# Tiles of the second norm, and the norm's small operations, in forms with two tensor sources on VectorE

## The chip, the core and the metric

The kernel runs on one core of a Trainium2 chip. The metric is the device time of one execution in microseconds (us), here the median of three: 321.2 us before the change, between 321.14 and 321.3. TensorE is called PE, VectorE DVE, ScalarE ACT, GpSimd POOL and SyncE SP.

## The reference, cut to what matters

Input: x (2 batches, 1024 tokens, 256 wide), a context of 64 tokens for each batch, and the weights of a gated cross-attention (16 heads of 64) and of a mixture of 8 experts, of which 2 are used for each batch.

```
x = x + tanh(g_xattn) * attention(layernorm(x), context)     # softmax over 64 context tokens, then Wo, bo
y = layernorm(x)                                             # mean, var over the 256 columns, eps 1e-5
logits = mean over tokens(y) @ gate_w ; the two best experts of each batch, weights renormalised
x = x + tanh(g_ffn) * sum over the 2 experts of w * (gelu(y @ w1[e] + b1[e]) @ w2[e] + b2[e])
```

## The kernel before, in words

All is float32 in the inputs. Each product on PE is split in a high and a low half (`_hi`, `_lo`, type fp32r) and done as three matmuls into the same sum (lines 1153 to 1155). The tokens lie in 16 tiles of 128; tile t of x is `xt[:, t, :]`, 128 partitions by 256 columns.

Every engine has its own list of instructions, in an order written out by hand, and the lists are tied by semaphores. The attention runs as a software pipeline of steps s (function `step` on each engine). In one step PE transposes the probabilities of tile s-2 (L1238), transposes a tile of y where there is one (L1326), computes the scores of tile s, and multiplies the transposed probabilities with the folded value weights (`ps<-vw`). From s = 3 on the residual of tile s-3 is added to x on DVE (L949), and `bn_stats` takes its statistics (L954).

POOL has three jobs in these steps: it multiplies the probabilities with the reciprocal of their sum (L504, two halves, PE waits for them before L1238), it normalises a later tile of x in two passes over `xs` (L522, L524), and it refines reciprocal square roots by Newton's iteration for most groups of tiles (`newton`, L470 to L476, thirteen small instructions, each waited for by the next). In steps 7, 11 and 15 this iteration stands ahead of L504 in POOL's list, in steps 1 and 4 behind it.

The change touches two functions of DVE:

- `norm` (its `0 in parts` block, lines 762 to 768, and the first guess at line 770) turns the two halves of `bn_stats` into mean and variance of a group of tiles: instructions on 128x4 or 128x8 elements. It is called seven times: three times for x (four, four and eight tiles) and four times for y (four tiles each). `link` puts a wait behind an instruction: DVE goes on only when that instruction has signalled. Behind `norm`, POOL is told to begin the Newton iteration, except in the first call for x and the last for y, where DVE does the iteration itself (L774 to L776).
- `y_tile` (line 969) writes y of one tile, (x - mean) * rstd, as one `tensor_scalar` with mean and rstd as per-partition scalars. It is called for the eight tiles of batch 0: one at the end of each of steps 7 to 10, two each at the end of steps 11 and 12. PE's transposes of that tile (L1326) wait for it. The eight tiles of batch 1 are done by POOL in two passes (L535, L538), and are not touched.

The only other `tensor_scalar` of this kind on DVE in the steps, `xn` at line 883, keeps its form. Neither do the experts' loops change: there DVE splits the gelu's output in two halves (L1112, L1114) and the next expert's weights (L1048, L1053).

Of the kernel before, what the change touches and what calls it, by code (L numbers as in the profile page):

```python
# [5 lines left out]
def gated_cross_attention_moe_kernel(nc, x, xT, ctx_tokens, g_xattn, g_ffn, Wq, Wk, Wv, Wo, bo,  # L6
# [5 lines left out]
    ALU = mybir.AluOpType  # L12
# [4 lines left out]
    P = 128  # L17
    B, M, D = ctx_tokens.shape
    S = out.shape[0] // B
    HD = 2 * Wv.shape[-1]  # L20
    DH = 64
    H = HD // DH
    E, _, F = w1.shape
    TOP = 2
    NT = B * S // P
# [10 lines left out]
    EPS = 1e-5  # L36
# [4 lines left out]
    def x_block(b, t0, t1):  # L41

        first = next(n for n, (part, u0, u1) in enumerate(_X_BLOCKS) if part == b and u0 <= t0 and t1 <= u1)
        assert _X_BLOCKS[first] == (b, t0, t1)
        start = sum(P * (u1 - u0) * D for _, u0, u1 in _X_BLOCKS[:first])
        return x[start:start + P * (t1 - t0) * D].rearrange("(p t d) -> p t d", p=P, d=D)
# [6 lines left out]
    def place(name, shape, dtype=f32, at=None):  # L53
        size = 4
        for n in shape[1:]:
            size *= n
        offset = cursor[0] if at is None else at[0]
        t = nc.alloc_sbuf_tensor_at(name, shape, dtype, offset=offset)
        (cursor if at is None else at)[0] = offset + (size + 31) // 32 * 32
        return t  # L60


    xt = place("xt", [P, NT, D])
# [3 lines left out]

    stats2 = stats1
    mean1 = place("mean1", [P, NT])
    rstd1 = place("rstd1", [P, NT])  # L70
    mean2 = place("mean2", [P, NT])
    rstd2 = place("rstd2", [P, NT])
# [67 lines left out]
    yb = place("yb", [P, 2, D], at=first3)  # L140
# [35 lines left out]
    with stack:  # L176
        ps = stack.enter_context(nc.psum_tensor("ps", [P, 8, BANK], f32))

        def sem(name):
            return stack.enter_context(nc.semaphore(name))  # L180
# [25 lines left out]
        y_ready, yT_done, yhi_ready, ylo_ready = (  # L206
            sem(n) for n in ("y_ready", "yT_done", "yhi_ready", "ylo_ready"))
        rep_ready, logits_done, idx_ready, gap_ready, gap_done, sel_ready = (
            sem(n) for n in ("rep_ready", "logits_done", "idx_ready", "gap_ready", "gap_done", "sel_ready"))
        stat_out, stat_in, xT_raw, xT_ready = (sem(n) for n in ("stat_out", "stat_in", "xT_raw", "xT_ready"))  # L210
        y_rstd, x_rstd, xn_by_dve, w1_first = sem("y_rstd"), sem("x_rstd"), sem("xn_by_dve"), sem("w1_first")
        staged_w1 = [sem("staged_w1_0"), sem("staged_w1_1")]
        staged_half = [sem("staged_half_0"), sem("staged_half_1")]
# [151 lines left out]
        def wait_pos(eng, s, v):  # L365

            if v > 0:
                eng.wait_ge(s, v)
# [375 lines left out]
        def _(dve):  # L744
            ln = [0]

            def link(ins):

                ln[0] += 1
                ins.then_inc(ln_step, 1)  # L750
                dve.wait_ge(ln_step, ln[0])

            def norm(t0, t1, mean, rstd, var, parts=range(4)):


                tiles, n = slice(t0, t1), t1 - t0
                me, ce, mo, co = (stats1[:, tiles, i] for i in (1, 2, 4, 5))
                m, r = mean[:, tiles], rstd[:, tiles]
                v, d, u = var[:, tiles], dm[:, 0:n], nu[:, 0:n]
                tt, ts, stt = nc.vector.tensor_tensor, nc.vector.tensor_scalar, nc.vector.scalar_tensor_tensor  # L760
                if 0 in parts:
                    tt(d, me, mo, ALU.subtract)
                    tt(m, me, mo, ALU.add)
                    link(tt(v, ce, co, ALU.add))
                    ts(m, m, 0.5, None, ALU.mult)
                    tt(d, d, d, ALU.mult)
                    link(ts(v, v, 1.0 / D, EPS, ALU.mult, ALU.add))
                    link(stt(v, d, 0.25, v, ALU.mult, ALU.add))

                    link(ts(r.bitcast(i32), v.bitcast(i32), -0.5, float(0x5F3759DF), ALU.mult, ALU.add))  # L770
                for part in (1, 2, 3):
                    if part in parts:

                        link(stt(u, v, -0.5, r, ALU.mult, ALU.mult))  # L774
                        link(tt(u, u, r, ALU.mult))
                        link(stt(r, u, 1.5, r, ALU.add, ALU.mult))  # L776
# [12 lines left out]
            def x_norm(i):  # L789

                t0, t1 = X_PARTS[i]
                dve.wait_ge(stats_done, stats_of[t1 - 1])
                norm(t0, t1, mean1, rstd1, ve_x, range(4) if i == 0 else (0,))
                dve.sem_inc(guess_ready, 1)

            def group(kind, i):
                n = number[(kind, i)]
                bank = ps[:, GRP_BANK[(kind, i)], :]
                if kind == "ctxT":
                    dve.wait_ge(grp_done, n + 1)  # L800
                    nc.vector.tensor_copy(ctxT[:, :, :], bank[:, 0:D].rearrange("p (k i) -> p k i", k=KD)).then_inc(grp_dve, 1)
                if kind == "vT":
                    dve.wait_ge(grp_done, n + 1)
                    nc.vector.tensor_copy(vT_sb[:, 4 * i:4 * i + 4, :, :].rearrange("p m b j -> p (m b j)"),
                                          bank).then_inc(grp_dve, 1)
                if kind == "A":
                    dve.wait_ge(grp_hi, HI_AT[(kind, i)])
                    nc.vector.tensor_tensor(a_part(a_lo, i), bank.rearrange("p (m b x) -> p m b x", m=4, b=B),
                                            as_f32(a_part(a_hi, i)), ALU.subtract).then_inc(grp_dve, 1)
                if kind == "VW":  # L810
                    dve.wait_ge(tg_ready, 1)
                    dve.wait_ge(grp_hi, HI_AT[(kind, i)])
                    nc.vector.scalar_tensor_tensor(vw[:, 2 * i:2 * i + 2, D:2 * D],
                                                   bank.rearrange("p (m n) -> p m n", m=2), tg[:, 0:1],
                                                   as_f32(vw[:, 2 * i:2 * i + 2, 0:D]), ALU.mult,
                                                   ALU.subtract).then_inc(grp_dve, 1)
# [13 lines left out]
                                        ALU.subtract).then_inc(xlo_ready, 1)  # L830

            nc.vector.memset(warm_w[:, :], 0.0).then_inc(warm_ready, 1)
            dve.sem_inc(hlo_ready, FREE_GELS)
            group("ctxT", 0)
            x_stats(0, range(0, 2))
# [12 lines left out]
            def step(s, par):  # L848
# [82 lines left out]
                for y in (Y_WITH_X.get(s + 1), Y_AFTER.get(s + 1)):  # L931
                    if y is not None:
                        y_tile(y)
# [24 lines left out]
            def y_guess(i):  # L958

                t0, t1 = Y_PARTS[i]  # L960
                dve.wait_ge(stats_done, stats_of[("x1", t1 - 1)])
                norm(t0, t1, mean2, rstd2, ve_y, range(4) if i == 3 else (0,))
                dve.sem_inc(guess_ready, 1)

            def y_tile(t):

                dve.wait_ge(y_rstd, t // 4 + 1)
                wait_pos(dve, yT_done, t - 1)
                nc.vector.tensor_scalar(yb[:, t % 2, :], xt[:, t, :], mean2[:, t:t + 1], rstd2[:, t:t + 1],
                                        ALU.subtract, ALU.mult).then_inc(y_ready, 1)  # L970

            def y_low(t, bank, c0, until):

# [550 lines left out]
```

## Time and profile before

| | |
|---|---|
| median of 3 runs | 321.2 us (321.14 to 321.3) |
| the profiled execution | 321.67 us, of which 319.7 us are the profiled span |
| PE busy | 313.2 us, 98% of the span |
| DVE busy | 236.5 us, 74%, 563 instructions |
| ACT, POOL busy | 164.6 us, 84.5 us |
| mean granted clock of PE | 0.999 |

Times in the rows are us from the span's start. A row of the timeline has the start, the busy time and the instruction; the names are output<-inputs. In brackets stands idle time of the engine ahead of it and who ended it. `xN` at the end means that N instructions are merged. A PE matmul's recorded time overlaps the next one's.

### The profile page before, as it was taken

The page shows a single profiled execution, that of the slowest core. Times are in us where ns is not written, and L with a number is a line of the kernel's source. Part 1 is how long each engine was busy: PE and PEld are TensorE (multiplying, and loading weights), DVE is VectorE, ACT ScalarE, POOL GpSimd, SP SyncE. Part 2 cuts the span into 40 slices and gives each one's busy share as a digit, 9 for nine tenths or more (in the row PEclk, how much of TensorE's full clock was granted, in tenths as well). Part 3 has the DMA queues.
Part 4 walks back from the last instruction along what each step waited for, and adds up shares of the span by engine and source line. Part 5 has one row for each costly group of instructions (what it writes and reads, how often), then busy time and mean ns, then how long its engine had stood idle before and what let it go on. Part 6 is the DMA issues. An engine that isn't in the chain of part 4 may idle for free.

```text
span 319.7 us, 5709 instructions
## 1 busy us (share of the span) xinstructions
PE 313.2 (98%) x1861; PEld 269.9 (84%) x1861; DVE 236.5 (74%) x563; ACT 164.6 (52%) x577; POOL 84.5 (26%) x158
## 2 busy tenths in 40 slices
PE   8999999999999999999999999999999999999996
PEld 7878998878988999888788888888887899888896
DVE  1889999989989999999998475466767554442643
ACT  2648565686766768766366254444543442321320
POOL 1325547586476655425600000000000000000000
PEclk9999999999999999999999999999999999999999
DMA  7997300300000009500016250000020000000012
GB/s 261 386 330 9 35 3 1 133 1 3 0 0 3 0 2 331 195 3 0 2 8 255 79 187 0 0 0 0 24 99 11 2 0 0 2 0 0 2 66 67
DMA packets 21918, 19.99 MB, mean 63 GB/s; under 512 B 11708, under 2 KB 17540, under 8 KB 21508
## 3 DMA queue, kind: packets, MB, share of 16 engines
q1 hardware_dynamic: 21616, 19.14, 19.9%
q10 hardware_dynamic: 276, 0.52, 0.4%
q8 instruction: 14, 0.23, 0.3%
q14 instruction: 12, 0.10, 0.1%
HBM read 17.56 MB, written 2.11 MB: 62 GB/s over the span
## 4 chain that ended last, share of the span: by engine, by line
PE 71%; POOL 10%; DVE 7%; issue 7%; DMA 2%; ACT 2%; SPq 0%; POOLq 0%; DVEq 0%
PE ps L1153 22%; PE ps L1154 22%; PE ps L1155 22%; POOL sx L504 4%; DMA xt<-in_x_dram 2%; POOL xs L524 2%; PE ps L1238 2%; POOL xs L522 2%; ACT sx L636 1%; DVE mx L903 1%; PE ps L1173 1%; DVE pT_lo L862 1%; PE ps L1326 1%; DVE sm L873 1%; PE ps L1424 1%
## 5 line engine op out<-in xcount | busy, mean ns | idle before, releaser
L723 ACT ACTIVATE gel<-ps,b1sel 128x512 f32<-128x512 f32 x64 | 43.9, 690 | 95.5 <-PE ps L1155 95.4
L1112 DVE CAST h_hi<-gel 128x512 fp32r<-128x512 f32 x64 | 28.4, 444 | 58.8 <-ACT gel L723 58.5
L636 ACT ACTIVATE sx<-ps,mx 128x64 f32<-128x64 f32 x128 | 38.3, 325 | 26.2 <-DVE mx L903 26.1
L1153 PE MATMUL ps<-yT_hi,w_hi 128*128 128x512 f32 (+1 forms) x128 | 50.5, 395 | 0.0
L1154 PE MATMUL ps<-yT_lo,w_hi 128*128 128x512 f32 (+1 forms) x128 | 50.0, 390 | 0.0
L1155 PE MATMUL ps<-yT_hi,w_lo 128*128 128x512 f32 (+1 forms) x128 | 49.9, 390 | 0.0
L1114 DVE TENSOR_TENSOR h_lo<-gel,h_hi 128x512 fp32r<-128x512 f32 x64 | 44.9, 702 | 2.2
L504 POOL TENSOR_TENSOR sx<-sx,rs 128x512 f32<-128x512 f32 x32 | 33.5, 1066 | 41.5 <-DVE rs L878 40.8
L1153 PE MATMUL ps<-h_hi,w_hi 128*128 128x512 f32 x96 | 38.4, 400 | 0.0
L1155 PE MATMUL ps<-h_hi,w_lo 128*128 128x512 f32 x96 | 37.5, 390 | 0.0
L1154 PE MATMUL ps<-h_lo,w_hi 128*128 128x512 f32 x96 | 37.4, 390 | 0.0
L1153 PE MATMUL ps<-vw,pT_hi 128*128 128x256 f32 x128 | 36.6, 286 | 0.1
L1155 PE MATMUL ps<-vw,pT_lo 128*128 128x256 f32 x128 | 36.2, 283 | 0.0
L1154 PE MATMUL ps<-vw,pT_hi 128*128 128x256 f32 x128 | 36.2, 283 | 0.0
L1155 PEld LDWEIGHTS ps<-yT_hi,w_lo 128*128 128x128 f32 x128 | 24.0, 188 | 5.1
L1153 PEld LDWEIGHTS ps<-yT_hi,w_hi 128*128 128x128 f32 x128 | 24.1, 188 | 4.6
L1154 PEld LDWEIGHTS ps<-yT_lo,w_hi 128*128 128x128 f32 x128 | 24.1, 188 | 4.4
L636 ACT ACTIVATION_READ_ACCUMULATOR sx<-ps,mx 128x1 f32 x128 | 27.8, 217 | 0.0
L1153 PE MATMUL ps<-a_hi,xT_hi 128*128 128x512 f32 x64 | 26.5, 413 | 0.1
L1153 PEld LDWEIGHTS ps<-vw,pT_hi 128*128 128x128 f32 x128 | 24.4, 191 | 2.0 <-issue 1.4
L1155 PE MATMUL ps<-a_hi,xT_lo 128*128 128x512 f32 x64 | 25.1, 392 | 0.0
L1154 PE MATMUL ps<-a_lo,xT_hi 128*128 128x512 f32 x64 | 25.0, 390 | 0.0
(149 smaller groups left out, 670.3 us busy)
## 6 DMA issues: line engine op xcount, KB each, us to landing
stage_w<-in_L_ffn_w_dram SPq DMA_DIRECT2D x7, 1024.0 KB, 7.4
out_dram<-xt SPq DMA_DIRECT2D x6, 256.0 KB, 2.3
wqT<-in_L_xattn_Wq_dram SPq DMA_DIRECT2D x2, 512.0 KB, 7.2
wv_sb<-in_L_xattn_Wv_dram SPq DMA_DIRECT2D x2, 512.0 KB, 8.8
wo_sb<-in_L_xattn_Wo_dram SPq DMA_DIRECT2D x1, 1024.0 KB, 13.9
xt<-in_x_dram SPq DMA_DIRECT2D x1, 1024.0 KB, 10.6
xs<-in_xT_dram SPq DMA_DIRECT2D x1, 1024.0 KB, 11.1
spread<-x_stat SPq DMA_DIRECT2D x1, 1024.0 KB, 4.6
```

Source lines behind the costliest of these rows:

```text
L504: nc.gpsimd.tensor_tensor(pr, pr, rs[:, q, hs].unsqueeze(2).broadcast_to([P, H // 2, M]), ALU.mult).then_inc(mul_done, 1)
L522: nc.gpsimd.tensor_tensor(x_raw(t), x_raw(t), mean, ALU.subtract).then_inc(xc_ready, 1)
L524: nc.gpsimd.tensor_tensor(x_raw(t), x_raw(t), rstd, ALU.mult).then_inc(xT_ready, 1)
L636: last = nc.scalar.activation(sx[:, par, c0:c0 + M], ps[:, 2 * par + 1, c0 - BANK:c0 - BANK + M], ACT.Exp, bias=mx[:, par, h:h + 1], accum ...
L723: nc.scalar.activation(gel[:, f % 4, :], ps[:, h_bank, :], ACT.Gelu, bias=b1sel[:, b, slot, f:f + 1]).then_inc(gelu_done, 1)
L862: nc.vector.tensor_tensor(pT_lo[:, par, 4 * half:4 * half + 4, :], ps[:, 4 + half, :].rearrange("p (m i) -> p m i", m=4), as_f32(pT_hi[:, ...
L1112: nc.vector.tensor_copy(h_hi[:, f % 4, :], gel[:, f % 4, :]).then_inc(hhi_ready, 1)
L1114: nc.vector.tensor_tensor(h_lo[:, f % 4, :], gel[:, f % 4, :], as_f32(h_hi[:, f % 4, :]), ALU.subtract).then_inc(hlo_ready, 1)
L1153: mm(acc, hi_w, hi_x, start=start, stop=False)
L1154: mm(acc, hi_w, lo_x, start=False, stop=False)
L1155: return mm(acc, lo_w, hi_x, start=False, stop=stop)
L1238: last = nc.tensor.transpose(ps[:, 4 + half, m * P:(m + 1) * P], sx[:, par, c0:c0 + P], ident[:, :])
```

## The change: what it does

1. A new tile `eps_col`, 128x1, is filled once with 1e-5 by a `memset` on DVE at the very start, behind the memset of `warm_w`, with a semaphore that DVE waits for.
2. In `norm`, the seven instructions of the block become six. The mean was made by an addition and a multiplication with 0.5; now it is me - 0.5 * d in one `scalar_tensor_tensor`, where d = me - mo is there already. The line that scales the variance and adds eps was a `tensor_scalar` with two constants; now it is a `scalar_tensor_tensor` whose second tensor is `eps_col`, broadcast. The square of d, which stood ahead of a link together with two others, now stands behind that link and has a link of its own: four links in place of three (with the one behind the first guess, not touched, five in place of four).
3. In `y_tile` the `tensor_scalar` becomes a `scalar_tensor_tensor`: the mean stays a per-partition scalar, rstd becomes a second tensor source, broadcast over the 256 columns.

```diff
                 if 0 in parts:
                     tt(d, me, mo, ALU.subtract)
-                    tt(m, me, mo, ALU.add)
                     link(tt(v, ce, co, ALU.add))
-                    ts(m, m, 0.5, None, ALU.mult)
-                    tt(d, d, d, ALU.mult)
-                    link(ts(v, v, 1.0 / D, EPS, ALU.mult, ALU.add))
+                    stt(m, d, -0.5, me, ALU.mult, ALU.add)
+                    link(stt(v, v, 1.0 / D, eps_col[:, 0:1].broadcast_to([P, n]), ALU.mult, ALU.add))
+                    link(tt(d, d, d, ALU.mult))
                     link(stt(v, d, 0.25, v, ALU.mult, ALU.add))
...
             nc.vector.memset(warm_w[:, :], 0.0).then_inc(warm_ready, 1)
+            nc.vector.memset(eps_col[:, :], EPS).then_inc(eps_ready, 1)
+            dve.wait_ge(eps_ready, 1)
             dve.sem_inc(hlo_ready, FREE_GELS)
...
-                nc.vector.tensor_scalar(yb[:, t % 2, :], xt[:, t, :], mean2[:, t:t + 1], rstd2[:, t:t + 1],
-                                        ALU.subtract, ALU.mult).then_inc(y_ready, 1)
+                nc.vector.scalar_tensor_tensor(yb[:, t % 2, :], xt[:, t, :], mean2[:, t:t + 1],
+                                               rstd2[:, t:t + 1].broadcast_to([P, D]), ALU.subtract,
+                                               ALU.mult).then_inc(y_ready, 1)
```

## Rows read from the trace of the kernel before

**Rows 1.** The page, part 1: busy us (share of the span) and instructions.
```profile
PE 313.2 (98%) x1861; PEld 269.9 (84%) x1861; DVE 236.5 (74%) x563; ACT 164.6 (52%) x577; POOL 84.5 (26%) x158
```

**Rows 2.** Waits of PE's weight loads: us in total, times, longest us.
```profile
PEld ps L1238 <- POOL sx L504: 2.3, 7, 0.6
PEld ps L1326 <- DVE yb L969: 0.5, 1, 0.5
```

**Rows 3.** Timeline of PE: places where it waited behind a norm.
```profile
13.56 1.16 PE L1195 MATMUL ps<-kT_sb,wqT 64*128 64x128 f32 x16 [0.62 <-DVE a_lo L808]
...
56.20 0.66 PE L1238 MATMUL ps<-ident,sx 128*128 128x128 f32 x4 [0.34 <-POOL sx L504]
...
99.52 0.66 PE L1238 MATMUL ps<-ident,sx 128*128 128x128 f32 x4 [0.34 <-POOL sx L504]
```

**Rows 4.** Timeline of DVE: one norm with POOL idle.
```profile
86.00 0.17 DVE L762 TENSOR_TENSOR dm<-stats 128x4 f32<-128x4 f32 x1
...
86.16 0.15 DVE L764 TENSOR_TENSOR ve_y<-stats 128x4 f32<-128x4 f32 x1
86.35 0.17 DVE L765 TENSOR_SCALAR mean<-mean 128x4 f32<-128x4 f32 x1
...
86.89 0.17 DVE L770 TENSOR_SCALAR rstd<-ve_y 128x4 int32<-128x4 int32 x1
```

**Rows 5.** Timeline of DVE and POOL: the norm that meets POOL's passes.
```profile
47.72 0.74 POOL L522 TENSOR_TENSOR xs<-xs,spread 128x256 f32<-128x256 f32 x1
48.54 0.75 POOL L524 TENSOR_TENSOR xs<-xs,spread 128x256 f32<-128x256 f32 x1
...
47.77 0.72 DVE L763 TENSOR_TENSOR mean<-stats 128x8 f32<-128x8 f32 x1
...
48.61 0.70 DVE L765 TENSOR_SCALAR mean<-mean 128x8 f32<-128x8 f32 x1
```

**Rows 6.** Timeline of POOL and DVE: a two-source instruction that meets a POOL pass.
```profile
151.51 0.68 POOL L538 TENSOR_TENSOR yb<-yb,rstd 128x256 f32<-128x256 f32 x1
...
151.75 0.98 DVE L1114 TENSOR_TENSOR h_lo<-gel,h_hi 128x512 fp32r<-128x512 f32 x1
```

**Rows 7.** The old form alone (timeline); the new form by source (ns min/median/max).
```profile
32.03 0.33 DVE L883 TENSOR_SCALAR xn<-xt,mean,rstd 128x256 f32<-128x256 f32 x1
...
L1053 DVE SCALAR_TENSOR_TENSOR w_lo<-stage_w,swt,w_hi x48: 340/344/695, 157.1 to 269.4; 128x128 fp32r<-128x128 f32 x32, - x16
...
L1034 DVE SCALAR_TENSOR_TENSOR w_lo<-stage_w,swt,w_hi x2: 1302/1470/1639, 137.5 to 148.2; 128x1024 fp32r<-128x1024 f32 x2
```

**Rows 8.** Timeline of DVE, POOL and PE: the first tile of y.
```profile
71.13 1.02 DVE L969 TENSOR_SCALAR yb<-xt,mean,rstd 128x256 f32<-128x256 f32 x1
71.15 0.85 POOL L522 TENSOR_TENSOR xs<-xs,spread 128x256 f32<-128x256 f32 x1
...
72.21 0.44 PE L1326 MATMUL ps<-ident,yb 128*128 128x128 f32 x2 [0.31 <-DVE yb L969]
```

**Rows 9.** Timeline of step 9: DVE's idle time, the tile, POOL's second pass.
```profile
79.78 1.29 DVE L862 TENSOR_TENSOR pT_lo<-ps,pT_hi 128x512 fp32r<-128x512 f32 x2 [0.58 <-ACT pT_hi L648]
...
84.33 0.84 DVE L969 TENSOR_SCALAR yb<-xt,mean,rstd 128x256 f32<-128x256 f32 x1
...
85.10 0.86 POOL L524 TENSOR_TENSOR xs<-xs,spread 128x256 f32<-128x256 f32 x1
```

**Rows 10.** Timeline of step 10: the tile, PE's transposes, POOL's iteration.
```profile
91.75 0.78 DVE L969 TENSOR_SCALAR yb<-xt,mean,rstd 128x256 f32<-128x256 f32 x1
...
92.68 0.41 PE L1326 MATMUL ps<-ident,yb 128*128 128x128 f32 x2
...
93.29 0.23 POOL L470 TENSOR_SCALAR ve_p<-ve_y 128x4 f32<-128x4 f32 x1
```

**Rows 11.** Timeline: the first tile of step 12, and PE behind it.
```profile
106.06 0.49 DVE L969 TENSOR_SCALAR yb<-xt,mean,rstd 128x256 f32<-128x256 f32 x1
...
106.94 0.38 PE L1326 MATMUL ps<-ident,yb 128*128 128x128 f32 x2
```

More of the change, by code:

```diff
@@ L69, in gated_cross_attention_moe_kernel @@
     mean1 = place("mean1", [P, NT])
+    eps_col = place("eps_col", [P, 1])
     rstd1 = place("rstd1", [P, NT])
@@ L210, in gated_cross_attention_moe_kernel @@
         stat_out, stat_in, xT_raw, xT_ready = (sem(n) for n in ("stat_out", "stat_in", "xT_raw", "xT_ready"))
+        eps_ready = sem("eps_ready")
         y_rstd, x_rstd, xn_by_dve, w1_first = sem("y_rstd"), sem("x_rstd"), sem("xn_by_dve"), sem("w1_first")
```

## The prediction

> **What bounds the kernel now.** The page's first part comes first: PE is busy for 313.2 of 319.7 us, DVE for 236.5, POOL for 84.5 [rows 1]. The kernel can only move where PE stands still, and an edit on DVE counts only where PE waits, directly or through POOL, for it. So the next view is who ends PE's waits. The weight loads wait for POOL's product with the reciprocal sums seven times, 2.3 us in total, and once, for 0.5 us, for a tile of y [rows 2]. The timeline gives the places. At 13.56 PE has idled 0.62 us for the split of the scores' weights, which DVE does behind the first norm; at 56.20 and 99.52 it has idled 0.34 us for L504, which POOL reached late because a Newton iteration stood ahead of it, and that iteration had waited for a norm of DVE's, or for POOL's passes beside a tile of y [rows 3]. At 72.21 PE has idled 0.31 us for the first tile of y [rows 8]. What falls ahead of 99.52 and on these chains moves the end one for one; behind it PE is nearly always busy with work in hand, and DVE has room.
>
> **Why a tile of y takes so long.** The same form, at line 883, takes 0.33 us when POOL is idle [rows 7]. The first tile takes 1.02: it begins at 71.13, POOL's L522 ends at 71.15 + 0.85 = 72.00, and the tile ends at 72.15 [rows 8]. It is held until POOL's pass is over, then needs 0.15 us. The new form is meant to be a different kind of reader. Is it held as well? The rows say yes. In the norm at 47.77 a plain addition with two SBUF sources, 8 columns wide, takes 0.72 us and ends at 48.49, POOL's pass at 47.72 + 0.74 = 48.46; the `tensor_scalar` at 48.61 takes 0.70 beside the next pass [rows 5]. Both forms are held alike. At 512 columns the two-source subtraction at 151.75 ends at 152.73, POOL's pass at 152.19: 0.54 us behind it, about 1.05 ns for each column [rows 6].
>
> For this the Trainium skill has a rule, in "SBUF — State Buffer", section "Who interferes with whom": a VectorE instruction with two SBUF inputs contends with a GpSimd instruction that reads SBUF, and the later one is blocked fully. It speaks against the change, and the trace agrees (0.72 us for 8 columns). The page "Advanced Engine Details and Errata", section "VectorE Performance Modes", names only the two-port modes as blocked; by that alone the new form would run free. That is the second rival below.
>
> **The tile's price.** Held, the old form ends 0.15 us behind POOL's pass. For the new one 256 columns at 1.05 ns are 0.27, with some 0.01 to 0.02 to begin, 0.28 in all: a held tile ends 0.13 us later. Free of POOL, `scalar_tensor_tensor` takes 0.340 at 128 columns and 1.302 at 1024 [rows 7], so 1.07 ns a column and 0.34 + 128 * 1.07 = 0.48 at 256, against 0.33: 0.15 more. The bounds are 0.13 to 0.15 if POOL's order stands; the far end below nothing is the first tile running free, 1.02 - 0.48 = 0.54 us less. I take 0.13, since every tile of y has POOL's passes beside it.
>
> **The norm's price.** Alone, its starts lie at 86.00 and 86.16, behind the link at 86.35, and the guess starts at 86.89 [rows 4]. Instructions that follow without a link start 0.08 apart, one behind a link 0.19 to 0.20. Before: two such gaps of 0.08, a link, two of 0.08, a link, a link: 0.89. After: one 0.08, a link, one 0.08, and three links (scaled variance, square, sum): 0.16 + 4 * 0.195 = 0.94. One instruction less, one link more: 0.05 later, each time; I take the new form at 4 or 8 columns to last like the others. Bounds: 0, if the scheduler hides one gap, and 0.12 in the norm that meets POOL: there the additions are still held to 48.49; if the mean is then held by the pass that starts at 48.54, the square starts only behind the held variance, near 49.4, and one more link follows. If the mean slips in ahead of that pass it is 0.05.
>
> **The memset** and its wait cost DVE no more than one small linked instruction, about 0.2 us [rows 4]. They lie at the very start, where DVE's next work is to copy the transposed context, for which it has to wait for a DMA and PE: nothing; uncovered it would be 0.2.
>
> **The sum, along the chain of waits.** Each term is how much later PE is from there on.
> - First norm for x: DVE runs straight from it into the splits that PE waits for at 13.56 [rows 3]: +0.05.
> - Second norm for x (four tiles): it stands in DVE's list ahead of the reciprocals, hence of POOL's L504, which PE waits for soon after: +0.05, 0.10.
> - Third norm for x (+0.05 to 0.12) feeds the wait at 56.20 [rows 3]; the first norm for y, on DVE behind it, feeds the next L504 by another path. The two lie beside each other, and PE takes about one of them: +0.05, 0.15.
> - First tile of y, for which PE waits at 72.21 [rows 8]: +0.13, 0.28.
> - Tile in step 8: DVE then idles 0.58 us for ACT before 79.78 [rows 9], which hides it. Nothing.
> - Tile at 84.33, whose end is followed without a gap by residual, statistics and the second norm for y [rows 9]: +0.13 and +0.05. This is late on DVE, 0.46, not yet on PE.
> - Tile at 91.75: it ends at 92.53, and PE's transposes begin at 92.68 [rows 10], a few hundredths or a tenth behind it, so PE becomes late with the tile: 0.46 + 0.13 = 0.59 at most. What counts more is POOL: its second pass beside that tile comes later by between 0 and 0.13 (at 85.10 it began before the tile had ended and lost nothing visible, 0.86 us [rows 9]); I take 0.05. Then comes the Newton iteration from 93.29 [rows 10], L504, and the wait at 99.52 [rows 3]: PE is late there by 0.46 + 0.05 = 0.51, and the 0.59 is swallowed by its idle time at that place.
> - The four tiles of steps 11 and 12 make DVE later than PE's 0.51 by 0.13 each. PE's transposes of the third of them begin at 106.94, the tile ends at 106.06 + 0.49 = 106.55 [rows 11]: room of 0.39, and three times 0.13 is 0.39. It just fits. I take nothing, at most 0.1.
> - The last norm for y runs with the experts' matmuls in hand: +0.05 on DVE, nothing on PE. POOL's tiles of batch 1 are unchanged.
>
> The sum is 0.05 + 0.05 + 0.05 + 0.13 + 0.13 + 0.05 + 0.05 = 0.51, say 0.5 us. On the profiled execution: 321.67 + 0.5 = 322.2 (span 320.2). That execution lies 0.5 above the median of three, 321.2, so the predicted median is 321.7. About 0.2%, 0.64 us, is what can be told from no change; the forecast lies just under it.
>
> **Rivals.**
> 1. *Backlog of the double tiles (slower).* Place: steps 11 and 12. If each tile costs 0.2 rather than 0.13, because the new form's longer start (0.34 us at 128 columns [rows 7]) shows as well, the three tiles make DVE later by 0.6, the room of 0.39 at 106.94 is passed by 0.21, and PE waits there again. It decides from 0.13 a tile on. Price: the two tiles in the sum give 0.14 more, the new wait 0.21: 0.86 in all, median 322.1. For it: there is no room to spare [rows 11]. Against it: behind a held start only the columns showed [rows 6].
> 2. *The new form isn't held (faster).* The first tile then takes 0.48 for 1.02 and PE's idle time of 0.31 at 72.21 is gone; the tile at 84.33 gains 0.84 - 0.48 = 0.36 [rows 9], and POOL's L504 before 99.52 comes earlier by it: -0.31 - 0.36 + 0.2 for four norms, about -0.5 us, median 320.7. Against it stand the held addition [rows 5] and subtraction [rows 6].
> 3. *The order of the two engines turns.* At 71.13 DVE came 0.02 us before POOL's L522 and lost [rows 8]. If a shift of hundredths lets it in first, the wait at 72.21 goes, but PE meets the waits at 92.68 and 99.52 instead, which give most of it back: -0.1 to +0.3, median 321.3.
>
> **How the numbers follow.** Forecast (+0.3 to +0.64, its own range 321.5 to 321.85) 0.45; turned order or norms costing nothing 0.20, of which nearly all is within 0.2%; backlog and anything dearer 0.27; not held 0.08, of which most would pass 0.2%. A tenth of the forecast's own chance lies past 0.64. Faster 0.07, same 0.61, slower 0.32. The range reaches into both neighbours, from 321.0 (norms at nothing, order turned) to 322.2 (backlog).
>
> **What would show it.** Tiles of y 0.13 us longer each, ending 0.28 behind a POOL pass; norms from first start to guess at 0.94; PE's wait for the first tile 0.13 longer; the wait at 99.52 still there, half a microsecond later; behind it the same number of us to the end. Wrong would be: tiles of y at 0.5 us beside POOL's passes; PE waiting for tile 6 or for the router's means; or a norm quicker than 0.89.

## The result: 0.25% slower, and the profile after

| | before | after |
|---|---|---|
| median, 15 runs each on one chip | 321.3 us (321.06 to 321.75) | 322.04 us (321.81 to 322.56) |
| ratio after / before, 95% interval | | 1.0025, 1.0017 to 1.0033 |
| profiled execution, span | 321.67 us, 319.7 us | 321.93 us, 320.1 us |

The median moved by 0.74 us where 0.5 was forecast: in the stated range (321.0 to 322.2), past the forecast's own upper end of 321.85, and just beyond the 0.2% (0.64 us) that can be told from no change. The page after, part 1 (columns as in [rows 1]):

```profile
PE 313.6 (98%) x1861; PEld 270.0 (84%) x1861; DVE 237.5 (74%) x557; ACT 164.4 (51%) x577; POOL 84.9 (27%) x158
```

DVE has six instructions less (seven norms with one less each, one memset more) and 1.0 us more of work. Who ends the waits of PE's weight loads, after, against [rows 2] (us in total, times, longest us):

```profile
PEld ps L1242 <- POOL sx L506: 1.9, 5, 0.6
...
PEld ps L1330 <- DVE yT_lo L979: 1.0, 4, 0.3
...
PEld ps L1330 <- DVE yb L972: 0.7, 1, 0.7
PEld ps L1330 <- issue: 0.6, 1, 0.6
```

The same view of before has two more lines for these transposes than [rows 2] shows:

```profile
PEld ps L1326 <- DVE yT_lo L975: 0.5, 2, 0.4
...
PEld ps L1326 <- issue: 0.3, 1, 0.3
```

The wait for a tile of y grew from 0.5 to 0.7, an unnamed one in front of the same transposes from 0.3 to 0.6 (it is the tile of step 10, below), and the waits for `yT_lo`, the low half of the transposed tile before, from 0.5 to 1.0 us. Idle times under 0.15 us stand in none of these lists. Line numbers after are two to four higher; L1330 is the old L1326.

**The tile.** Timeline after, against [rows 8]:

```profile
70.87 1.15 DVE L972 SCALAR_TENSOR_TENSOR yb<-xt,mean,rstd 128x256 f32<-128x256 f32 x1
70.89 0.85 POOL L524 TENSOR_TENSOR xs<-xs,spread 128x256 f32<-128x256 f32 x1
...
72.07 0.44 PE L1330 MATMUL ps<-ident,yb 128*128 128x128 f32 x2 [0.43 <-DVE yb L972]
```

POOL's pass ends at 71.74, the tile at 72.02, 0.28 us behind it; before, it was 0.15. PE's idle time is 0.43 for 0.31. The same in step 9, against [rows 9]: pass to 84.88, tile to 85.18 by the rounded rows (0.29 us apart unrounded), and the norm that follows.

```profile
83.95 0.93 POOL L524 TENSOR_TENSOR xs<-xs,spread 128x256 f32<-128x256 f32 x1
84.20 0.98 DVE L972 SCALAR_TENSOR_TENSOR yb<-xt,mean,rstd 128x256 f32<-128x256 f32 x1
84.97 0.93 POOL L526 TENSOR_TENSOR xs<-xs,spread 128x256 f32<-128x256 f32 x1
86.00 0.17 DVE L764 TENSOR_TENSOR dm<-stats 128x4 f32<-128x4 f32 x1
...
86.36 0.15 DVE L767 SCALAR_TENSOR_TENSOR ve_y<-ve_y,eps_col 128x4 f32<-128x4 f32 x1
86.55 0.16 DVE L768 TENSOR_TENSOR dm<-dm 128x4 f32<-128x4 f32 x1
...
86.94 0.17 DVE L771 TENSOR_SCALAR rstd<-ve_y 128x4 int32<-128x4 int32 x1
```

The norm takes 0.94 us from first start (86.00) to guess (86.94), 0.89 in [rows 4]. In the norm that meets POOL's passes, against [rows 5], the mean starts at 48.15, 0.01 ahead of the second pass, and gets through; the scaled variance, now with `eps_col` as a second tensor, doesn't:

```profile
48.15 0.17 DVE L766 SCALAR_TENSOR_TENSOR mean<-dm,stats 128x8 f32<-128x8 f32 x1
48.23 0.72 DVE L767 SCALAR_TENSOR_TENSOR ve_x<-ve_x,eps_col 128x8 f32<-128x8 f32 x1
```

In step 10 PE waits for the tile as well. It did so before too, which [rows 10] doesn't show: the weight loads (first line below) idled 0.29 us and began 0.12 behind the tile's end at 92.53. After, they idle 0.62 and begin at 92.82, again 0.12 behind the tile's end (92.71); PE's own row names the tile now.

```profile
92.64 0.20 PEld L1326 LDWEIGHTS ps<-ident,yb 128*128 128x128 f32 x2 [0.29 <-issue]
```

```profile
91.81 0.90 DVE L972 SCALAR_TENSOR_TENSOR yb<-xt,mean,rstd 128x256 f32<-128x256 f32 x1
...
92.85 0.41 PE L1330 MATMUL ps<-ident,yb 128*128 128x128 f32 x2 [0.41 <-DVE yb L972]
```

**Where PE lost it.** The same matmuls were paired in the two traces, and their starts subtracted. How much later each is than before, counted from the wait at 13.56 (which itself came 0.41 us earlier in this execution; see the last section):

| place in the trace before | forecast, from 13.56 on | after | tile_only | norm_only |
|---|---|---|---|---|
| 27.47, product for PE | 0.05 | 0.05 | 0.01 | 0.03 |
| 63.38, product | 0.10 | 0.17 | 0.01 | 0.15 |
| 72.21, first tile of y | 0.23 | 0.28 | 0.13 | 0.14 |
| 92.68, tile of step 10 | 0.54 | 0.59 | 0.39 | 0.19 |
| 99.52, product behind the iteration | 0.46 | 0.46 | 0.26 | 0.19 |
| 104.04, tile 5 | 0.46 | 0.70 | 0.50 | 0.21 |
| 111.01, tile 7 | 0.46 | 0.93 | 0.74 | 0.19 |
| last matmul, 316.57 | 0.46 | 0.90 | 0.73 | 0.15 |

The first norm lies ahead of 13.56. From the start of the second block of x's statistics (8.34 before, 7.88 after) to this wait it is 5.22 us before and 5.26 after, 5.23 in tile_only: 0.04 for the first norm, 0.94 in all up to the last matmul. The block itself began 0.46 earlier, which leaves the 0.48 by which the profiled span grew.

Up to 99.52 the sum holds, with 0.05 to 0.07 too much on the way. Behind it the forecast had nothing, and there is 0.44: 0.24 at tile 5, 0.05 more by 106.94, 0.18 more at tile 7, and 0.03 given back by the end. Timeline after, then before, of tile 5:

```profile
103.86 0.41 DVE L979 TENSOR_TENSOR yT_lo<-ps,yT_hi 128x256 fp32r<-128x256 f32 x1
...
104.32 0.20 PEld L1330 LDWEIGHTS ps<-ident,yb 128*128 128x128 f32 x2 [0.29 <-DVE yT_lo L979]
104.33 0.44 PE L1330 MATMUL ps<-ident,yb 128*128 128x128 f32 x2
```

```profile
103.54 0.41 DVE L975 TENSOR_TENSOR yT_lo<-ps,yT_hi 128x256 fp32r<-128x256 f32 x1
...
104.00 0.20 PEld L1326 LDWEIGHTS ps<-ident,yb 128*128 128x128 f32 x2
```

PE's transposes of tile 5 overwrite the half bank from which DVE still takes the low half of tile 4, so they wait for it. After, DVE is through at 104.27, and the loads begin 0.05 behind it, after 0.29 us of idle time. Before, DVE was through at 103.95, and the loads began at 104.00, 0.05 behind it as well: no idle time, but no room either. At 111.01 the same holds for tile 7 and the low half of tile 6. After, DVE is through at 111.47, the loads come at 111.52 with 0.25 idle. Before, they were waiting already: DVE was through at 110.95, the load ahead had ended at 110.92, and 0.08 us of idle time is too short for the lists.

```profile
111.06 0.41 DVE L979 TENSOR_TENSOR yT_lo<-ps,yT_hi 128x256 fp32r<-128x256 f32 x1
...
111.52 0.20 PEld L1330 LDWEIGHTS ps<-ident,yb 128*128 128x128 f32 x2 [0.25 <-DVE yT_lo L979]
```

```profile
110.54 0.41 DVE L975 TENSOR_TENSOR yT_lo<-ps,yT_hi 128x256 fp32r<-128x256 f32 x1
...
110.73 0.19 PEld L1155 LDWEIGHTS ps<-vw,pT_lo 128*128 128x128 f32 x1
...
111.00 0.20 PEld L1326 LDWEIGHTS ps<-ident,yb 128*128 128x128 f32 x2
```

### The profile page after: what moved, and what is told of

Its sections match the earlier page's. It is cut to its first block, busy times and chain, and to the rows that moved or that the text cites. A ratio compares the mean times of both kernels' runs of the same rounds, so it can differ in the third digit from the quotient of the medians.

```text
span 320.1 us, 5703 instructions
## 1 busy us (share of the span) xinstructions
PE 313.6 (98%) x1861; PEld 270.0 (84%) x1861; DVE 237.5 (74%) x557; ACT 164.4 (51%) x577; POOL 84.9 (27%) x158
## 4 chain that ended last, share of the span: by engine, by line
PE 67%; DVE 21%; ACT 5%; issue 4%; DMA 2%; SPq 0%; DVEq 0%
PE ps L1157 21%; PE ps L1158 21%; PE ps L1159 21%; DVE mx L906 4%; DVE pT_lo L865 4%; ACT sx L638 4%; DVE sm L876 3%; DMA xt<-in_x_dram 2%; DVE yb L972 2%; DVE xT_lo L897 1%; DVE vw L814 1%; PE ps L1177 1%; PE ps L1242 1%; ACT pT_hi L650 1%; PE ps L1428 1%
## 5 line engine op out<-in xcount | busy, mean ns | idle before, releaser
L506 POOL TENSOR_TENSOR sx<-sx,rs 128x512 f32<-128x512 f32 x32 | 33.5, 1066 | 41.9 <-DVE rs L881 41.2
```

The costliest lines, as they stand in the source:

```text
L506: nc.gpsimd.tensor_tensor(pr, pr, rs[:, q, hs].unsqueeze(2).broadcast_to([P, H // 2, M]), ALU.mult).then_inc(mul_done, 1)
```

## The experiments

Times are medians; the kernel before was run beside each group on the same chip. "On the path" is the lateness of the last matmul counted from 13.56, as in the table. It is read from one profile of each kernel; column_only, whose instructions are those of before, shows its scatter: 0.05, and up to 0.09 on the way.

| run | median, us | before beside it | ratio (95%) | on the path |
|---|---|---|---|---|
| tile_only | 322.43 | 321.69 | 1.0018 (1.0009 to 1.0026) | +0.73 |
| norm_only | 321.34 | 321.69 | 0.9989 (0.9979 to 0.9999) | +0.15 |
| y_later | 322.03 | 321.69 | 1.0012 (0.9996 to 1.0029) | +0.66 |
| y_later_old_forms | 321.38 | 321.69 | 0.9991 (0.9974 to 1.0008) | -0.08 |
| column_only | 321.46 | 321.43 | 1.0001 (0.9992 to 1.0011) | -0.05 |
| norm_no_column | 321.53 | 321.43 | 1.0004 (0.9995 to 1.0013) | +0.23 |
| norm_short | 320.92 | 321.43 | 0.9986 (0.9977 to 0.9995) | -0.22 |
| tiles_on_act | 324.39 | 321.43 | 1.0090 (1.0075 to 1.0106) | +3.25 |
| tile_before_exp | 321.50 | 321.66 | 0.9994 (0.9985 to 1.0003) | -0.07 |
| tile_before_exp_short | 320.88 | 321.66 | 0.9975 (0.9965 to 0.9984) | -0.55 |
| pool_cut_old, pool_cut_new (one run each) | 320.1, 320.1 | 321.66 | | -1.67, -1.35 |

pool_cut_old and pool_cut_new leave out work and compute something else, so their times are no gain.

The theory at the start: the tile is held by POOL's passes and pays its 256 columns behind them, the norms pay a link each, and DVE's backlog of the double tiles reaches PE at tiles 5 and 7. The rivals: the norms carry it, or the late waits are only moved work.

**tile_only**: the change's third part alone.
```diff
-                nc.vector.tensor_scalar(yb[:, t % 2, :], xt[:, t, :], mean2[:, t:t + 1], rstd2[:, t:t + 1],
-                                        ALU.subtract, ALU.mult).then_inc(y_ready, 1)
+                nc.vector.scalar_tensor_tensor(yb[:, t % 2, :], xt[:, t, :], mean2[:, t:t + 1],
+                                               rstd2[:, t:t + 1].broadcast_to([P, D]), ALU.subtract,
+                                               ALU.mult).then_inc(y_ready, 1)
```


> Only the eight tiles of y on VectorE take the form with two tensor sources; the norms are as before. Theory (a held two-source tile streams its 256 columns behind GpSimd's pass at one column a cycle, 0.28 us, where the old form needed 0.15): +0.13 at the first tile, +0.13 to 0.2 by step 11, and about 0.4 more where TensorE transposes the second tile of steps 12 and 13: +0.5 to +0.7 us over the kernel before. Rival (the norms carry most of it): +0.1 to +0.3 us.

+0.74 us by the medians, +0.73 on the path: 0.26 by 99.52 and 0.47 behind it. The tile's form is about four fifths of the loss on the path.

**norm_only**: the change without its third part.


> Only the norm's small operations change (six instructions, five links in all, eps from a column); the tiles of y keep the old form. Theory: each norm lasts 0.05 us longer from its first start to the guess (0.94 against 0.89), four of them lie on the chain: +0.1 to +0.25 us. Rival (the two-source forms on 4 columns are dear, or meet GpSimd more often): +0.4 us or more.

On the path +0.15, inside the expectation. By the medians it is 0.35 us faster, outside of it, with an interval that reaches almost to no change. norm_no_column and column_only, below, show no such gain, so nothing speaks for the norm's order or the column alone as its cause; the memset with its wait, and eps as a tensor, were not tried by themselves. The two halves add up on the path: 0.73 + 0.15 = 0.88, against 0.90 for the change.

**y_later** and, as its control, **y_later_old_forms**: the change, and the kernel before, with PE's transposes of tiles 5 and 7 one block later.
```diff
-                        if m == 3 and s in Y_AFTER:
+                        if m == 4 and s in Y_AFTER:
```


> The whole change, and TensorE's transposes of the second tile of a step (tiles 5 and 7) stand one block of three matmuls later in its list (behind block 4 of 8 in place of block 3; 0.36 us). Theory (0.47 us of the loss is TensorE waiting there for VectorE's backlog): most of it comes back, the time is 0.3 to 0.45 us below the changed kernel, so +0.3 to +0.45 over the kernel before. Rival (the wait only moves to the next product): less than 0.1 us below the changed kernel, +0.65 or more over the kernel before.

> The kernel before with the same later place of the transposes of tiles 5 and 7, as a control. Theory: TensorE did not wait there before, so nothing changes, within 0.1 us. Rival (a later place is worth something by itself): 0.2 us faster or more.

Behind 99.52 the changed kernel loses 0.17 on the path instead of 0.44 (0.66 - 0.49), so the later place removes 0.27 of it. The old forms change by -0.08, as much as the idle time that stood at 111.00 before; of the 0.44 that the change had added, then, only some 0.19 goes. That is more than the rival allows on the path (0.24 below the changed kernel) and less than the theory's 0.3 to 0.45. The rest was passed on: counted from 99.52, PE is 0.11 later when it transposes tile 6, where it now waits for the tile itself (DVE is through at 107.05), and it loses another tenth by the router's matmuls.

```profile
107.17 0.20 PEld L1330 LDWEIGHTS ps<-ident,yb 128*128 128x128 f32 x2 [0.17 <-issue]
```

The intervals of the timed runs (1.0012, against 1.0025 for the change, measured in another group) are too wide to tell 0.27 us.

**column_only** and **norm_no_column**: what the 0.35 us of norm_only were.
```diff
     mean1 = place("mean1", [P, NT])
+    eps_col = place("eps_col", [P, 1])
```
In column_only nothing fills or reads this column. norm_no_column has the new order and eps as a constant:
```diff
-                    tt(m, me, mo, ALU.add)
                     link(tt(v, ce, co, ALU.add))
-                    ts(m, m, 0.5, None, ALU.mult)
-                    tt(d, d, d, ALU.mult)
+                    stt(m, d, -0.5, me, ALU.mult, ALU.add)
                     link(ts(v, v, 1.0 / D, EPS, ALU.mult, ALU.add))
+                    link(tt(d, d, d, ALU.mult))
```


> The kernel before with the one unused column placed where the change places it, so that every tile behind it lies 32 or 64 bytes further in SBUF; nothing fills or reads it. In the profiles so far the second block of x's statistics began at 7.88 to 7.97 us in the three kernels with the column, at 8.15 to 8.39 in the three without. Theory (the place in SBUF moves the first loads): x's second block is there 0.2 to 0.4 us earlier and the kernel is 0.2 to 0.4 us faster than before. Rival (chance of single profiles): no change, within 0.1 us.

> The norm's new order (mean from the difference, square behind a link of its own) with eps as a constant and no column, tiles of y as before. Theory: norms of 0.94 us against 0.89, TensorE 0.15 to 0.2 us later at the end, and no earlier start: +0.1 to +0.25 us over the kernel before. Rival (the norms are harmless, and the 0.35 us gained with the column was theirs): 0.2 to 0.4 us faster.

The times don't bear out the theory of the place in SBUF: with the column alone the ratio is 1.0001 (0.9992 to 1.0011). Its profile has x's second block early nevertheless, at 7.95, and norm_no_column without a column has it at 8.00; the last section has the other kernels. The reordered norm costs +0.23 on the path; its timed interval, 0.9995 to 1.0013, holds both that and nothing.

**norm_short**: the mean from the difference, but the square goes to a tile of its own and stays in front of the old link.
```diff
-                    tt(m, me, mo, ALU.add)
                     link(tt(v, ce, co, ALU.add))
-                    ts(m, m, 0.5, None, ALU.mult)
-                    tt(d, d, d, ALU.mult)
+                    stt(m, d, -0.5, me, ALU.mult, ALU.add)
+                    tt(u, d, d, ALU.mult)
                     link(ts(v, v, 1.0 / D, EPS, ALU.mult, ALU.add))
-                    link(stt(v, d, 0.25, v, ALU.mult, ALU.add))
+                    link(stt(v, u, 0.25, v, ALU.mult, ALU.add))
```


> The norm with the mean from the difference, but the square of the difference goes to a tile of its own (nu, free at that point) and stays in front of the same link as the scaled variance: six instructions, one link less than the change. Tiles of y as before. Theory (a norm costs its gaps: 0.08 us an instruction, 0.2 a link): 0.81 us against 0.89, five norms on the chain, -0.2 to -0.35 us. Rival (only the number of links counts, four here as before): no change.

0.51 us faster by the medians, -0.22 on the path, to which the first norm's 0.07 ahead of 13.56 comes. The rest of the 0.51 has no cause that was found. Both are on the theory's side. Its norm in step 10, with POOL idle, takes 0.82 us to the guess, 0.89 in [rows 4]:

```profile
85.51 0.17 DVE L762 TENSOR_TENSOR dm<-stats 128x4 f32<-128x4 f32 x1
...
85.94 0.16 DVE L766 TENSOR_SCALAR ve_y<-ve_y 128x4 f32<-128x4 f32 x1
...
86.33 0.17 DVE L769 TENSOR_SCALAR rstd<-ve_y 128x4 int32<-128x4 int32 x1
```

The norm of the change saves the same gap of 0.08 us, but the link of its own makes another gap 0.2 in place of 0.08.

**tiles_on_act**: the eight tiles on ScalarE, ahead of the exponentials of the same step.
```diff
+                nc.scalar.activation(yb[:, t % 2, :], xt[:, t, :], ACT.Identity, bias=ve_x[:, TB + t:TB + t + 1],
+                                     scale=rstd2[:, t:t + 1]).then_inc(y_ready, 1)
```


> The eight tiles of y go to ScalarE (identity with scale rstd and bias -mean * rstd, made by two small operations of one column), ahead of the exponentials of the same step; VectorE has none. Norms as before. Theory (VectorE loses 0.5 to 0.7 us a tile to GpSimd's passes, and TensorE waits for it at 72.2, 92.7 and 99.5): those waits go, 0.5 to 1.0 us faster than before. Rival (ScalarE's exponentials become late in their place, and VectorE waits for them): no gain, or slower by up to 0.5 us.

POOL doesn't hold these: all eight last 0.60 us, the six that overlap a POOL operation like the two that don't. The gain came, 0.48 us at 72.21, and then the rival, far beyond its 0.5: 3.25 us slower at the end. Timeline of ACT in step 11; tile 4 can't be begun before POOL's iteration is through, and the exponentials stand behind it:

```profile
97.07 0.20 ACT L628 ACTIVATE ve_x<-mean 128x1 f32<-128x1 f32 x1 [1.38 <-POOLq L482]
...
97.63 0.60 ACT L636 ACTIVATE yb<-xt,ve_x,rstd 128x256 f32<-128x256 f32 x1
98.14 0.30 ACT L653 ACTIVATE sx<-ps,mx 128x64 f32<-128x64 f32 x1
```

PE is at +1.28 by tile 5 and at +3.22 by tile 7. Which part is the 1.1 us of each tile and which the order was not taken apart.

**tile_before_exp** and **tile_before_exp_short**: old forms; the first tile of a step one place earlier in DVE's list, ahead of L910; the second with the short norm too.
```diff
+                if Y_WITH_X.get(s + 1) is not None:
+                    y_tile(Y_WITH_X[s + 1])
                 t = s
                 if active(t):
                     dve.wait_ge(max_done, t + 1)
...
-                for y in (Y_WITH_X.get(s + 1), Y_AFTER.get(s + 1)):
-                    if y is not None:
-                        y_tile(y)
+                if Y_AFTER.get(s + 1) is not None:
+                    y_tile(Y_AFTER[s + 1])
```


> Old forms everywhere; VectorE writes a step's (first) tile of y ahead of the subtraction of the maxima, while GpSimd still has the second product with the reciprocals in hand, and no longer behind it. Theory (the tile's price is the wait for a GpSimd pass, and the end of a nearer pass comes sooner): the tiles that PE waits for at 72.2 and 92.7 come 0.5 us or more earlier, and most of the 0.5 us at 72.2 is gained: 0.2 to 0.7 us faster than before. Rival (the exponentials and the residual behind it become late by as much): no change or slower.

> The same with the short norm (mean from the difference, square in a tile of its own, four links). Theory: the two gains lie on one chain and add up: 0.2 us faster than tile_before_exp, 0.4 to 0.9 us faster than before. Rival: one hides the other, no faster than the better of the two.

Alone it gains 0.42 us at the transposes of 72.21 and loses most of it at the next product, where the weight loads now wait for `vw`, which stands behind L910 in DVE's list; a second gain, 0.33 at 92.68, is gone by 99.52 (0.00). So the rival came about, not the theory's 0.2 to 0.7.

```profile
72.30 0.19 PEld L1154 LDWEIGHTS ps<-a_hi,xT_hi 128*128 128x128 f32 x1 [0.38 <-DVE vw L813]
```

With the short norm the kernel is 0.78 us faster than before, ratio 0.9975 (0.9965 to 0.9984), as expected (0.4 to 0.9), the fastest of the kernels that compute everything; against norm_short alone (0.9986, 0.9977 to 0.9995) the intervals overlap. On the path it is -0.55, where the two parts have -0.22 and -0.07: more than their sum, and why was not followed up. In step 9 of this kernel the tile ends at 84.18, 0.15 behind POOL's product with the reciprocals (81.93 + 2.10 = 84.03), and one pass earlier than before, so it lasts 0.67 for 0.84 [rows 9]:

```profile
81.93 2.10 POOL L504 TENSOR_TENSOR sx<-sx,rs 128x512 f32<-128x512 f32 x2 [2.94 <-DVE rs L877]
...
83.51 0.67 DVE L969 TENSOR_SCALAR yb<-xt,mean,rstd 128x256 f32<-128x256 f32 x1
83.99 0.97 POOL L522 TENSOR_TENSOR xs<-xs,spread 128x256 f32<-128x256 f32 x1
```

**pool_cut_old** and **pool_cut_new**: POOL's two passes over tiles 6 to 15 of x cut to 4 of 128 tokens in each half, so that the rest of those tiles isn't normalised.
```diff
-                nc.gpsimd.tensor_tensor(x_raw(t), x_raw(t), mean, ALU.subtract).then_inc(xc_ready, 1)
+                nc.gpsimd.tensor_tensor(x_raw(t)[:, :, 0:4], x_raw(t)[:, :, 0:4], mean[:, :, 0:4], ALU.subtract).then_inc(xc_ready, 1)
...
-                nc.gpsimd.tensor_tensor(x_raw(t), x_raw(t), rstd, ALU.mult).then_inc(xT_ready, 1)
+                nc.gpsimd.tensor_tensor(x_raw(t)[:, :, 0:4], x_raw(t)[:, :, 0:4], rstd[:, :, 0:4], ALU.mult).then_inc(xT_ready, 1)
```


> The whole change with GpSimd's two passes over a tile of x (from tile 6 on) cut from 128 to 4 tokens in each half, so that the rest of xs isn't normalised; GpSimd's passes are then short. Theory (what a tile of y costs is the wait for a pass): the tiles of y in the new form last 0.45 to 0.55 us where no product with the reciprocals is beside them. Rival (the new form itself is slow): 0.8 us or more, as with the passes.

> The kernel before with the same cut passes (the rest of xs isn't normalised). Theory: tiles of y at 0.33 to 0.4 us where nothing holds them, 0.15 us shorter than the new form; the distance between the two kernels is smaller than with the passes, 0.2 to 0.5 us. Rival: 0.8 us as with the passes.

By source (ns min/median/max), the cut kernels with the new and with the old form, then the change and the kernel before as they are:

```profile
L972 DVE SCALAR_TENSOR_TENSOR yb<-xt,mean,rstd x8: 472/477/524, 70.5 to 105.2; 128x256 f32<-128x256 f32 x8
```
```profile
L969 DVE TENSOR_SCALAR yb<-xt,mean,rstd x8: 401/405/408, 70.5 to 104.9; 128x256 f32<-128x256 f32 x8
```
```profile
L972 DVE SCALAR_TENSOR_TENSOR yb<-xt,mean,rstd x8: 628/1020/1145, 70.9 to 106.9; 128x256 f32<-128x256 f32 x8
```
```profile
L969 DVE TENSOR_SCALAR yb<-xt,mean,rstd x8: 491/882/1019, 71.1 to 106.5; 128x256 f32<-128x256 f32 x8
```

Without the passes both forms are less than half as long, and the forms differ by 0.07 us, half of the 0.15 expected; behind a pass they differ by 0.13. The two kernels then end 0.32 us apart on the path, where it was 0.90.

## Why the prediction was right, and where it was short

- *Held alike.* Right, and the trace before was enough to say so: the tiles of the new form end 0.28 us behind the GpSimd operation that they met, in all eight cases to within 0.01 (72.02 behind 71.74).
- *The tile's price, 0.13.* Right for a held tile. The price free of POOL was too high: 0.07, not 0.15 (0.477 as estimated, but the old form lasts 0.405 in this place, not the 0.33 of line 883).
- *The norm's price, 0.05, and 0.05 to 0.12 where it meets POOL.* 0.94 for 0.89, as said. Where it meets POOL it takes 2.10 for 2.01, since the scaled variance is held in the mean's place. The first norm shows as 0.04 ahead of 13.56. Behind it the path has 0.15 (norm_only) and 0.23 (norm_no_column) for the norms, against 0.15 forecast with the one in step 10.
- *The memset, nothing.* Right: it ends at 1.00, and DVE's next work, the copy of the context, idles 3.82 us for PE after it.
- *The sum to 99.52.* Forecast 0.46 from 13.56 on, measured 0.46. Its parts are off by a few hundredths each: the tiles have 0.26 (tile_only) where 0.31 was forecast, so the 0.05 for POOL's second pass didn't show, and the norms 0.19 where 0.15 was. The idle time at 99.52 swallowed 0.13, 0.08 in the forecast.
- *"It just fits. I take nothing, at most 0.1."* This step failed. It compared DVE's lateness with one wait, that for tile 6 at 106.94. What PE reaches first is the wait for `yT_lo` ahead of tiles 5 and 7. There was no room there: at 104.00 the loads began as soon as DVE's end let them, and at 111.00 they had idled 0.08 us already. So DVE's two dearer tiles of each step came through. The price was 0.24, 0.05 and 0.18 one after the other, 0.44 at the end; a later place of the transposes took 0.27 away, of which some 0.08 had been there before. The view of before that [rows 2] comes from has a line for `yT_lo`, though for two later places of the run. The room of 0.39 at 106.94 was too large as well: it runs to PE's matmul, while the loads come at 106.83 and, where PE did wait for a tile (step 10), began 0.12 behind its end, which leaves 0.17. In y_later that was used up.
- *The range.* That the median lies in it is owed to its upper end, which the first rival gave. That rival has the mechanism in outline (DVE's backlog of the double tiles reaches PE), but not what made up its 0.86: tiles in the sum at 0.14 more, which they weren't, and a wait of 0.21 at 106.94, which didn't arise. The 0.44 at other places makes nearly the same number by chance. The profiled span, forecast as 320.2 and measured as 320.1, is luck too: 0.94 lost behind the start of x's second block, less the 0.46 by which this start was earlier.
- *The order of the two engines.* At 70.87 and 70.89 DVE came 0.02 ahead and lost again, as before; the third rival did not come about. This pair doesn't test the order, since POOL's operation ahead (L506) ran to 70.93. tile_before_exp has a cleaner one: POOL had idled 0.18 us, DVE began 0.05 ahead of it by the records, and its tile was held nevertheless, to 0.15 behind POOL's end (70.33 behind 70.18, unrounded).

```profile
69.08 1.25 DVE L970 TENSOR_SCALAR yb<-xt,mean,rstd 128x256 f32<-128x256 f32 x1
...
69.13 1.04 POOL L504 TENSOR_TENSOR sx<-sx,rs 128x512 f32<-128x512 f32 x1 [0.18 <-POOL rstd L476]
```

## What to carry to other kernels

An instruction of VectorE that is held by GpSimd's access costs the wait for its end plus its own columns; here the form with two tensor sources was held just as the form with one. Between two such forms only the second part changes; the first changes with the place in the list. When an engine becomes later by a few tenths, list every wait of the critical engine for it, those that show no idle time too, with the room of each, measured to the start of the weight loads and less the 0.05 to 0.12 us that lay between DVE's end and the load where PE did wait. A wait that cost nothing before may have no room at all. And count small operations as gaps, 0.08 us for one more in a row, 0.2 for one more link.

## What the runs showed that was not expected

The first part of the kernel begins at a different moment in each profile. The second block of x's statistics starts with the landing of a DMA; three kernels whose work up to there is alike but for a memset in the second (before, the change, the unused column):

```profile
8.34 0.75 DVE L785 BATCH_NORM_STATS2 stats<-xt 128x6 f32<-128x256 f32 x2 [1.22 <-DMA xt<-in_x_dram]
```
```profile
7.88 0.75 DVE L786 BATCH_NORM_STATS2 stats<-xt 128x6 f32<-128x256 f32 x2 [1.21 <-DMA xt<-in_x_dram]
```
```profile
7.95 0.75 DVE L786 BATCH_NORM_STATS2 stats<-xt 128x6 f32<-128x256 f32 x2 [1.31 <-DMA xt<-in_x_dram]
```

Between before and the change this is 0.46 us, half of the effect that was to be explained, and it is why the profiled span grew by only 0.48 us. Over the profiles of all fourteen kernels the block starts between 7.88 and 8.44. The five with the column have 7.88 to 7.97, the nine without it 8.00 to 8.44, so a part of the column in it is not ruled out; but there is one profile of each, and the medians of column_only show no gain. It doesn't always pass through to PE either: in y_later_old_forms the block is 0.19 earlier than before, and the wait at 13.56 comes 0.11 later, since there PE's own work ahead of it starts 0.46 later. norm_only's gain of 0.35 us by the medians has no other cause that was found; it is not shown that the start is it. For differences this small, a comparison of the same matmuls counted from behind the first loads told more than the medians did, down to its own scatter of 0.05 to 0.1 us.
